# Interleaving VectorE's small dependent operations, and moving a mask sum and a residual sum to TensorE and ScalarE

## The chip, the cores and the metric

The kernel runs on one core of a Trainium2 chip. The metric is the device time of one execution in microseconds (us), lower is better. The core has TensorE (PE, with its weight loads shown as PEld), VectorE (DVE), ScalarE (ACT), GpSimd (POOL) and the DMA queue of SyncE (SP). Each engine works through its own list in order; between engines, and between dependent instructions of one engine, there are semaphores.

## The reference, cut to what matters

One adaptive-layernorm block over 16 images of 256 positions and 128 channels, all in float32:

```
h  = layernorm(x) * (1 + ca) + sa
x  = x + ga * attn(h)          # 8 heads, 33 samples around a position that the data chooses, linear interpolation
h2 = layernorm(x) * (1 + cb) + sb
logits = h2 @ router_w.T + router_b ; mask = the two largest of 8 experts
ffn = sum over chosen experts of (h2 @ expert_w[e] + expert_b[e])
x  = x + gb * ffn
```

The interpolated gather of `attn` is done as a matrix A (256 x 256 for each head and image) that VectorE builds, TensorE transposes and TensorE multiplies with h.

## The kernel before

**Units.** The 16 images are handled in nine units: one image, seven times two images, one image. `UNITS` holds them; `tiles(n)` is the number of 128-row tiles of unit n (4 for two images, 2 for one), `before(n)` the images ahead of it, `NU` = 9, `LAST` = 8, `LATE` = 7. Each engine's program is one list written out by hand: a loop over i, in which `run(i, lag, stage)` issues the stage of unit i + lag, and `second(...)` does so where the unit has two images. So in one turn of the loop three units are in work: unit i+1 is at its front (layernorm, projection, `line`, `ends_of`, `products`, `grid`), unit i in the middle (`network`, `spread_out`, `mid_A`), and units i-1 and i-2 at the back (gate and first residual, router, experts, last sum).

**VectorE in one turn.** `network` (six predicated copies that shift the rows of T by a data-dependent distance, L751) with `sum_ends` (L776) after the second copy and `masked` (hm, the expert masks times h2T, L849) and `residual` (x += gate, L805) between later ones; then for unit i+1 `line` (L694 to L702: `sums`, `f`, `lp`, `invf`, `nlf`), `ends_of` (L707 to L717: `lpe`, `fe`, `kap`) and `products` (L764, four instructions); then `spread_out(i, 0)`: two large products into AT (L788) and a small copy of the end cells (L796); `grid` (L726 to L738: `eI`, `sc`, `mask`, `sf`, `near`) of unit i+1; `route` of unit i-1 (L814 to L830: `lg`, four `max`, four `max_index`, `hit`, `mk`); `spread_out(i, 1)`; and `total(i-2)` (L854), which adds the expert result in PSUM to x.

**TensorE in one turn.** Transposes of AT (`mid_A`, L974) into four banks that ScalarE empties (L488), for image 1 of unit i-1 and then image 0 of unit i; `mid_attend` (L988); the projection rows (L946, L951); `mid_y` (L998), `mid_gate` (L1004); the experts (L1054); `back_x2T` (L1014), `back_logits` (L1025); `back_out` (L1076: transposes of the gated expert result moeT into bank pE); `back_mk` (L1031: transposes of the mask mk into pL). The end of the list, for image 0:

```python
run(i, -1, back_x2T)
run(i, -1, back_logits)
run(i, 0, mid_A, 0, 0)
run(i, -2, back_out)
run(i, 0, mid_A, 0, 1)
run(i, -1, back_mk)
run(i, 0, mid_attend, 0, 0)
run(i, 0, mid_attend, 0, 1)
```

**ScalarE in one turn.** `mid_A(i-1, 1)` (eight evictions), h^T of unit i+1 (L414), the cells c, the row activations and y between one another, then squares, sums, `front_u` (L453, waits for `nlf`), `norm2(i-1)` (L391), `back_h2T(i-1)` (L521), `back_moe(i-2)` (L537), `squares1`, `mid_A(i, 0)` (eight evictions), `back_mk(i-1)` (L530), `norm1(i+2)`.

SyncE's list has, in each turn, `masks` (the mask rows to DRAM and back, spread over 128 partitions) and `store` (a unit of x to the output), which waits for the last sum.

Of the kernel before, what the change touches and what calls it, by code (L numbers as in the profile page):

```python
# [49 lines left out]
def constants():  # L50
# [14 lines left out]
    c["erow"] = np.broadcast_to(np.arange(E, dtype=np.float32), (P, E)).copy()  # L65
# [11 lines left out]
    "late": (P, [("erow", E), ("owT", P), ("rwT", E), ("weT", E * P)]),  # L77
# [4 lines left out]
def build(nc, t):  # L82

    ctx = ExitStack()
    with ctx:
# [67 lines left out]
        hit = sb("hit", [P, BT, 2, E]); mk = sb("mk", [P, BT, NP * E])  # L153
# [29 lines left out]
        v_sum = sem("v_sum"); v_fp = sem("v_fp"); v_inv = sem("v_inv"); v_lin = sem("v_lin"); a_u = sem("a_u"); a_uR = sem("a_uR")  # L183
# [7 lines left out]
        v_top = sem("v_top"); v_topi = sem("v_topi"); v_hit = sem("v_hit"); v_mk = sem("v_mk")  # L191
        t_mk = sem("t_mk"); a_mk = sem("a_mk"); t_mb = sem("t_mb"); v_hm = sem("v_hm")
        t_moe = sem("t_moe"); a_moe = sem("a_moe"); t_out = sem("t_out"); v_out = sem("v_out")
# [65 lines left out]
        def _(sp):  # L259
# [84 lines left out]
        def _(act):  # L344
# [194 lines left out]

            for i in range(-2, LAST):  # L540
# [27 lines left out]
                run(i, -1, back_mk)  # L568
                run(i, 2, norm1)
# [21 lines left out]
        def _(dve):  # L591
# [96 lines left out]
            def line(n):  # L688
# [3 lines left out]
                if n == 0:  # L692
# [3 lines left out]
                nc.vector.tensor_scalar(f[:, 0:w], sums[:, 0:w, 0], FREQ_T / H, FREQ_MID, ALU.mult, ALU.add)  # L696
                nc.vector.scalar_tensor_tensor(lp[:, 0:w], sums[:, 0:w, 1], PHASE / H, lcol[:, 0:w], ALU.mult,
                                               ALU.add).then_inc(v_fp, 1)
                dve.wait_ge(v_fp, n + 1)
                nc.vector.reciprocal(invf[:, 0:w], f[:, 0:w]).then_inc(v_inv, 1)  # L700
# [108 lines left out]
            def route(n):  # L809
# [7 lines left out]
                for bt in range(w):  # L817
                    ins = nc.vector.max(top[:, bt, :], lg[:, bt, :])
# [368 lines left out]
```

## Time and profile before

| | |
|---|---|
| time, median of 3 runs | 310.94 us (309.18 to 311.23) |
| the profiled execution | 308.9 us, its span 307.0 us |
| busy in the span: DVE, PE, ACT, POOL | 277.2 (90%), 257.3 (84%), 229.4 (75%), 38.8 (13%) us |
| the chain that ended last, by engine | DVE 50%, PE 22%, issue 14%, ACT 11% |
| mean granted TensorE clock | 0.898 |

The profile is of one execution. The span runs from its first to its last instruction; 1.9 us of the device time lie outside it. TensorE's busy time is modelled and includes overlap of pipelined matmuls, so it isn't a measure of how full TensorE is.

### The profile page before, as it was taken

To read this page: it belongs to the slowest core of one execution; us is meant where nothing else is said; L and a number is where in the kernel's file an instruction comes from. 1 tells how busy PE (TensorE), PEld (TensorE's weight loads), DVE (VectorE), ACT (ScalarE), POOL (GpSimd) and SP (SyncE) were. 2 spreads that over 40 slices of the span, in tenths; PEclk is the share of its full clock that TensorE was granted. 3 is DMA by queue.
4 is the path that set the end of the run, shared out by engine and by line. 5 is a ranking of instruction groups with operands and counts; after the bars stand their busy time and mean duration, and the time that the engine had idled before them with its cause. 6 is when DMAs were issued, how large, how long until landed. Compare 5 with 4: busy or idle time off the path is not lost.

```text
span 307.0 us, 5136 instructions
## 1 busy us (share of the span) xinstructions
PE 257.3 (84%) x1720; PEld 189.1 (62%) x1720; DVE 277.2 (90%) x570; ACT 229.4 (75%) x636; POOL 38.8 (13%) x64
## 2 busy tenths in 40 slices
PE   6970971999489998999699989999899959888995
PEld 3530830874388477857597568747784758475664
DVE  7799988999979899999999999999999999991772
ACT  3585788799868998898869988998679656845301
POOL 6204001200410011002020011002200400001100
PEclk9596697599958999899969997999699989999999
DMA  5630000020002200140005000500003000400001
GB/s 170 206 97 0 2 0 0 0 71 1 1 2 61 96 1 0 36 138 3 0 1 174 0 0 2 168 8 1 0 37 137 2 1 20 155 0 2 26 9 53
DMA packets 12160, 12.91 MB, mean 42 GB/s; under 512 B 1171, under 2 KB 11110, under 8 KB 11366
## 3 DMA queue, kind: packets, MB, share of 16 engines
q1 hardware_dynamic: 11684, 12.18, 12.8%
q10 hardware_dynamic: 450, 0.40, 0.5%
q8 instruction: 14, 0.23, 0.3%
q14 instruction: 12, 0.10, 0.1%
HBM read 10.43 MB, written 2.15 MB: 41 GB/s over the span
## 4 chain that ended last, share of the span: by engine, by line
DVE 50%; PE 22%; issue 14%; ACT 11%; POOL 2%; DVEq 0%; ACTq 0%; POOLq 0%
DVE AT L788 18%; DVE T L751 12%; PE pT L974 4%; DVE hm L849 4%; PE pR L974 3%; PE pY L1054 3%; ACT c L471 2%; DVE x L805 2%; PE pE L1054 2%; ACT xn L391 2%; DVE endw L776 2%; PE pR L951 2%; DVE x L854 1%; ACT hT L414 1%; DVE prodF L764 1%
## 5 line engine op out<-in xcount | busy, mean ns | idle before, releaser
L751 DVE COPY_PREDICATED T<-mask,T 128x672 f32<-128x672 int16 (+11 forms) x54 | 83.3, 1543 | 0.8
L788 DVE TENSOR_TENSOR AT<-T,c 128x2064 f32<-128x2064 f32 x32 | 72.3, 2301 | 0.0
L488 ACT ACTIVATE A<-pT 128x512 f32<-128x512 f32 x64 | 36.1, 599 | 27.6 <-PE pT L974 27.1
L974 PE MATMUL pT<-first,AT 128*128 128x128 f32 x256 | 43.9, 328 | 13.1 <-DVE AT L796 13.0
L1054 PE MATMUL pE<-hm,late 128*128 128x256 f32 x224 | 52.6, 386 | 0.0
L974 PEld LDWEIGHTS pT<-first,AT 128*128 128x128 f32 x256 | 37.3, 173 | 17.2 <-DVE AT L796 15.5
L1054 PEld LDWEIGHTS pE<-hm,late 128*128 128x128 f32 x224 | 41.2, 190 | 6.6
L974 PE MATMUL pR<-first,AT 128*128 128x128 f32 x256 | 40.4, 311 | 0.0
L315 POOL TENSOR_SCALAR ve<-sq 128x4 f32<-128x4 f32 (+1 forms) x18 | 8.8, 487 | 245.8 <-ACT xn L361 202.2
L488 ACT ACTIVATE A<-pR 128x512 f32<-128x512 f32 x64 | 35.8, 611 | 3.7 <-PE pR L974 3.6
L974 PEld LDWEIGHTS pR<-first,AT 128*128 128x128 f32 x256 | 36.0, 165 | 0.0
L988 PE MATMUL pY<-A,hs 128*32 128x256 f32 x512 | 31.7, 384 | 0.2
L391 ACT ACTIVATE xn<-x,nm,rs 128x128 f32<-128x128 f32 x64 | 26.4, 480 | 5.1 <-POOL nm L319 5.1
L849 DVE TENSOR_TENSOR hm<-mkb,h2T 128x2048 f32<-128x2048 bf16 x13 | 29.7, 2284 | 0.0
L951 PE MATMUL pR<-proj,hT 128*128 128x297 f32 x64 | 25.5, 482 | 1.2 <-ACT hT L414 1.2
L471 ACT ACTIVATE c<-near,early 128x172 f32<-128x172 f32 (+1 forms) x54 | 26.0, 568 | 0.0
L988 PEld LDWEIGHTS pY<-A,hs 128*32 128x32 f32 x512 | 14.1, 109 | 13.1 <-ACT A L488 5.7
L361 ACT ACTIVATE xn<-x,mu 128x128 f32<-128x128 f32 x52 | 20.2, 390 | 0.5
L317 POOL TENSOR_TENSOR rs<-ve,mhalf 128x4 f32<-128x4 f32 (+1 forms) x18 | 19.8, 1102 | 1.5
L1014 PE MATMUL pX<-first,xn 128*128 128x128 f32 x32 | 6.1, 314 | 13.6 <-ACT xn L391 13.6
L426 ACT ACTIVATE T<-pR 128x297 f32<-128x297 f32 x32 | 13.8, 431 | 3.4 <-PE pR L951 3.4
L1025 PE MATMUL pL<-late,h2T 128*128 128x8 f32 x60 | 9.8, 289 | 7.7 <-ACT h2T L521 7.7
(139 smaller groups left out, 370.9 us busy)
## 6 DMA issues: line engine op xcount, KB each, us to landing
mkb<-mask_rows SPq DMA_DIRECT2D x6, 1024.0 KB, 5.4
x<-in_x SPq DMA_DIRECT2D x7, 256.0 KB, 5.6
out<-x SPq DMA_DIRECT2D x7, 256.0 KB, 5.7
late<-in_late SPq DMA_DIRECT2D x1, 584.0 KB, 3.9
mkb<-mask_rows SPq DMA_DIRECT2D x1, 512.0 KB, 3.8
x<-in_x SPq DMA_DIRECT2D x2, 128.0 KB, 3.5
wmod<-in_wmod ACTq DMA_DIRECT2D x1, 256.0 KB, 3.6
out<-x SPq DMA_DIRECT2D x2, 128.0 KB, 3.3
```

The costliest lines, as they stand in the source:

```text
L317: nc.gpsimd.tensor_tensor(rs[:, 0:w], ve[:, 0:w], mhalf[:, 0:w], ALU.pow).then_inc(out, 1)
L361: ins = nc.scalar.activation(junk[:, bt, :], of_x(n)[:, bt, :], ACT.Square, bias=mu[:, bt:bt + 1], accum_out=sq[:, bt:bt + 1])
L391: ins = nc.scalar.activation(xn[:, bt, :], of_x(n)[:, bt, :], ACT.Identity, bias=nm[:, bt:bt + 1], scale=rs[:, bt:bt + 1])
L471: nc.scalar.activation(cells[:, :, :, r], near[:, 0:w, :], ACT.Abs, bias=off[:, r:r + 1]).then_inc(a_abs, 1)
L488: nc.scalar.activation(A[b][:, m, 2 * j:2 * j + 2, :].rearrange("p h l -> p (h l)"), four_banks(k)[:, :], ACT.Copy).then_inc(a_A, 1)
L751: nc.vector.copy_predicated(rows[:, :, :, j0:j1], spread(mask[:, k, 0:w, j0:j1], [P, w, H, j1 - j0], 2), rows[:, :, :, j0 + (1 << bit):j1 ...
L788: nc.vector.tensor_tensor(AT[:, bt, :, :].rearrange("p h (j r) -> p h j r", r=BLK), spread(T[n % 2][:, bt, 0:H, 0:NB], [P, H, NB, BLK], 3) ...
L849: nc.vector.tensor_tensor(hm[b][:, :, :], mkb[n % 2][:, :, b * L:(b + 1) * L], spread(own, [P, E, L], 1), ALU.mult).then_inc(v_hm, 1)
L951: mm(dst, hT[:, bt * P:(bt + 1) * P], proj[:, :], start=False, stop=True).then_inc(t_row, 1)
L974: ins = nc.tensor.transpose(four_banks(k)[:, c0:c0 + P], AT[:, 2 * b + i, 2 * j + a, m * P:(m + 1) * P], ident)
L988: ins = mm(pY[32 * j:32 * j + 32, b * L:(b + 1) * L], hs[n % 2][:, 2 * b + m, hh, :], A[b][:, m, hh, :], start=(m == 0 and a == 0), stop=( ...
L1054: ins = mm(dst, weT[:, e, :], hm[b][:, e, :], start=False, stop=(e == E - 1))
```

## The change

Three things, and two series of matmuls that write nothing of use:

- **VectorE's order.** `line` takes `lpe` and `fe` in between and `invf` waits only for `f`; `grid` becomes `places`, `moves`, `stage_masks`, `offset`, `cells_from`, `route` becomes `logits`, `best`, `hits`, and the pieces of the two alternate; `spread_out` is issued tile by tile and its end copy (`set_ends`) comes one instruction later; `sum_ends` is cut in two around the second copy of `network`.
- **Hits on TensorE.** `hit` is written in three copies (24 columns in place of 8, so 128x192 elements for four tiles in place of 128x64), the addition `mk` goes, and TensorE's `back_mk` adds the two hits of a tile in the bank: two plain float32 matmuls against the identity for each tile in place of one transpose.
- **The last sum in the bank**, for units 0 to 5: `back_out` multiplies the identity with x into the bank and adds the transposed moeT there, two plain float32 matmuls for each tile in place of one transpose. ScalarE then copies the bank to x (a new `total`), and `store` and the next use of the bank wait for that copy. Units 6 to 8 keep VectorE's `total`.
- **Extra matmuls** in the loop from i = 1: four of bf16 128 x 512 between `back_x2T` and `back_logits`, two after `back_logits`, all into bank pT0, which nothing reads before `mid_A` rewrites it.

```diff
             def back_mk(n):
-                pe.wait_ge(v_mk, n + 1)
+                pe.wait_ge(v_hit, n + 1)
                 for bt in range(tiles(n)):
-                    ins = nc.tensor.transpose(pL[0:NP * E, bt * P:(bt + 1) * P], mk[:, bt, :], ident)
+                    for k in range(2):
+                        ins = mm(pL[0:NP * E, bt * P:(bt + 1) * P], hit[:, bt, k, :], ident,
+                                 start=(k == 0), stop=(k == 1))
                 ins.then_inc(t_mk, 1)
...
             def back_out(n):
                 pe.wait_ge(a_moe, before(n + 1))
                 for bt in range(tiles(n)):
-                    ins = nc.tensor.transpose(moe_bank(n)[:, bt * P:(bt + 1) * P], moeT[:, bt * P:(bt + 1) * P], ident)
+                    dst = moe_bank(n)[:, bt * P:(bt + 1) * P]
+                    if n < LATE - 1:
+                        pe.wait_ge(v_x2, n + 1)
+                        mm(dst, ident, of_x(n)[:, bt, :], start=True, stop=False)
+                        ins = mm(dst, moeT[:, bt * P:(bt + 1) * P], ident, start=False, stop=True)
+                    else:
+                        ins = nc.tensor.transpose(dst, moeT[:, bt * P:(bt + 1) * P], ident)
                 ins.then_inc(t_out, 1)
...
                 run(i, -1, back_x2T)
+                if i > 0:
+                    warm_up(4, pT[0])
                 run(i, -1, back_logits)
+                if i > 0:
+                    warm_up(2, pT[0])
                 run(i, 0, mid_A, 0, 0)
...
+            def total(n):                      # ScalarE
+                act.wait_ge(t_out, n + 1)
+                nc.scalar.activation(of_x(n), moe_bank(n)[:, 0:tiles(n) * C].rearrange("p (a c) -> p a c", c=C),
+                                     ACT.Copy).then_inc(a_out, 1)
...
                 run(i, -1, back_mk)
+                run(i, -2, total)
                 run(i, 2, norm1)
...
-                run(i, 0, network, range(0, 2))
+                run(i, 0, network, range(0, 1))
...
-                run(i, 0, sum_ends)
+                run(i, 0, sum_ends, 0)
+                run(i, 0, network, range(1, 2))
+                run(i, 0, sum_ends, 1)
                 run(i, 0, network, range(2, 4))
...
                 run(i, 1, line)
+                run(i, 1, past_ends)
                 run(i, 1, ends_of)
-                run(i, 1, products)
+                run(i, 1, product, 0, 0)
+                run(i, 1, product, 0, 1)
+                run(i, 1, product, 1, 0)
+                run(i, 1, product, 1, 1)
                 run(i, 0, spread_out, 0)
-                run(i, 1, grid)
-                run(i, -1, route)
-                second(i, 0, spread_out, 1)
-                run(i, -2, total)
+                run(i, 0, spread_out, 1)
+                run(i, 1, places)
+                run(i, 0, set_ends, 0)
+                run(i, 1, moves)
+                run(i, -1, logits)
+                run(i, 1, stage_masks)
+                run(i, -1, best)
+                run(i, 1, offset)
+                run(i, -1, hits)
+                second(i, 0, spread_out, 2)
+                second(i, 0, spread_out, 3)
+                run(i, 1, cells_from)
+                second(i, 0, set_ends, 1)
```

## Rows read from the trace of the kernel before

**Rows 1.** The page, part 1: busy us (share of the span) xinstructions.

```profile
PE 257.3 (84%) x1720; PEld 189.1 (62%) x1720; DVE 277.2 (90%) x570; ACT 229.4 (75%) x636; POOL 38.8 (13%) x64
```

**Rows 2.** Busy time by windows: stretch, length, engines, PEclk, DMA share, GB/s.

```profile
82.50:115.40 32.90, 29.50 (x198) 22.57 (x199) 29.77 (x59) 28.51 (x81) 2.87 (x6) 0.84 0.11 37
115.40:148.20 32.80, 30.88 (x217) 23.21 (x216) 32.22 (x61) 29.48 (x85) 4.13 (x6) 0.95 0.14 41
148.20:181.10 32.90, 29.46 (x205) 22.23 (x204) 32.31 (x61) 28.77 (x83) 3.17 (x6) 0.90 0.14 41
...
246.10:270.00 23.90, 19.64 (x164) 15.40 (x165) 23.45 (x38) 15.55 (x35) 0.00 (x0) 0.93 0.18 57
```

**Rows 3.** DVE's waits: us in total, times, longest us.

```profile
DVE lg L814 <- PE pL L1025: 8.1, 2, 6.4
```

**Rows 4.** DVE's timeline, one turn: start us, us, line, operation.

```profile
152.70 0.20 DVE L796 COPY AT<-endw 128x32 f32<-128x32 f32 x1
...
155.85 0.22 DVE L825 TENSOR_TENSOR hit<-late,topi 128x64 f32<-128x64 f32 x1
156.11 0.26 DVE L830 TENSOR_TENSOR mk<-hit 128x96 f32<-128x96 f32 x1
156.28 4.52 DVE L788 TENSOR_TENSOR AT<-T,c 128x2064 f32<-128x2064 f32 x2
...
160.94 0.69 DVE L854 TENSOR_TENSOR x<-pE,x 128x512 f32<-128x512 f32 x1
161.53 2.85 DVE L751 COPY_PREDICATED T<-mask,T 128x672 f32<-128x672 int16 x2
...
173.05 0.28 DVE L805 SCALAR_TENSOR_TENSOR x<-pY,x 128x128 f32<-128x128 f32 x1
...
178.00 0.18 DVE L696 TENSOR_SCALAR f<-sums 128x4 f32<-128x4 f32 x1
178.10 0.15 DVE L697 SCALAR_TENSOR_TENSOR lp<-sums,early 128x4 f32<-128x4 f32 x1
178.28 0.18 DVE L700 RECIPROCAL invf<-f 128x4 f32<-128x4 f32 x1
...
181.01 2.31 DVE L788 TENSOR_TENSOR AT<-T,c 128x2064 f32<-128x2064 f32 x1
```

**Rows 5.** PE's timeline, the same turn and the next one's start.

```profile
152.96 1.97 PE L974 MATMUL pT<-first,AT 128*128 128x128 f32 x8 [0.92 <-DVE AT L796]
...
156.43 1.06 PE L1076 MATMUL pE<-first,moeT 128*128 128x128 f32 x4
...
159.83 0.60 PE L1031 MATMUL pL<-first,mk 128*24 128x128 f32 x4
...
160.36 1.93 PE L988 MATMUL pY<-A,hs 128*32 128x256 f32 x32
...
162.22 1.09 PE L974 MATMUL pT<-first,AT 128*128 128x128 f32 x8
...
171.79 0.66 PE L1004 MATMUL pY<-first,y 128*128 128x128 f32 x4 [0.70 <-ACT y L510]
...
184.12 1.06 PE L1025 MATMUL pL<-late,h2T 128*128 128x8 f32 x8 [1.11 <-ACT h2T L521]
```

**Rows 6.** ACT's timeline, the same turn and the next one's start.

```profile
162.98 1.09 ACT L488 ACTIVATE A<-pT 128x512 f32<-128x512 f32 x2 [0.27 <-PE pT L974]
...
183.05 1.02 ACT L521 ACTIVATE h2T<-pX,modT 128x256 f32<-128x256 f32 x2 [0.75 <-PE pX L1014]
```

**Rows 7.** Busy time by windows, finer; the clock is the third number from the end.

```profile
156.40:158.04 1.64, 1.64 (x10) 1.64 (x9) 1.64 (x1) 0.61 (x2) 0.00 (x0) 0.50 0.00 0
158.04:159.68 1.64, 1.64 (x13) 1.64 (x12) 1.64 (x2) 1.12 (x3) 0.00 (x0) 0.73 0.00 0
```

**Rows 8.** PE's timeline, the end of the span.

```profile
285.13 0.61 PE L1031 MATMUL pL<-first,mk 128*24 128x128 f32 x4
```

**Rows 9.** PE's timeline, start: the nine extra matmuls that stand there.

```profile
13.12 3.31 PE L913 MATMUL pE<-warm 128*128 128x512 bf16 x9
```

More of the change, by code:

```diff
@@ new lines, in places, with moves @@
+            def places(n):
+                w = tiles(n)
+                dve.wait_ge(a_uR, n + 1)
+                nc.vector.scalar_tensor_tensor(eI[:, 0:w, :], uR[:, 0:w, :], ROUND, jcol[:, 0:w, :], ALU.subtract,
+                                               ALU.add).then_inc(v_eI, 1)
+            def moves(n):
+                nc.vector.tensor_scalar(sc[:, 0:tiles(n), :], uR[:, 0:tiles(n), 0:NB], ROUND, -float(HALF), ALU.subtract,
+                                        ALU.max).then_inc(v_sc, 1)
@@ L721, in grid, with stage_masks @@
+            def stage_masks(n):
                 w = tiles(n)
@@ L769, in sum_ends, with product @@
-            def sum_ends(n):
+            def product(n, q, far):
+                if q == 0 and not far:
+                    dve.wait_ge(v_kap, n + 1)
+                    dve.wait_ge(a_row, LT * before(n + 1))
+                own = slice(q, tiles(n), LT)
+                prod, count = ((prodN, END), (prodF, FAR))[far]
+                side = (q + far) % 2
+                c0 = SHIFT[q] + (S - count if side else 0)
+                nc.vector.tensor_tensor(
+                    prod[:, own, :, :], T[n % 2][:, own, 0:H, c0:c0 + count],
+                    spread(kap[:, own, side, 0:count], [P, UNITS[n][1], H, count], 2), ALU.mult).then_inc(v_prod, 1)
@@ L770, in sum_ends @@
+            def sum_ends(n, far):
                 w = tiles(n)
-                dve.wait_ge(v_prod, n + 1)
+                dve.wait_ge(v_prod, 4 * (n + 1))
+                if n > 0:
+                    dve.wait_ge(v_end, before(n))
                 cells = endw[:, 0:w, :, :].rearrange("p (b t) e h -> p b (t e) h", t=LT)
-                for own, prod in ((slice(0, 4, 3), prodN), (slice(1, 3), prodF)):
-                    src = prod[:, 0:w, :, :].rearrange("p (b t) h s -> p b t h s", t=LT)
-                    ins = nc.vector.tensor_reduce(cells[:, :, own, :], src, AX.X, ALU.add)
@@ L777, in sum_ends, with spread_out @@
-                ins.then_inc(v_endw, 1)
-            def spread_out(n, b):
-                img = before(n) + b
-                if b == 0:
+                own, prod = ((slice(0, 4, 3), prodN), (slice(1, 3), prodF))[far]
+                src = prod[:, 0:w, :, :].rearrange("p (b t) h s -> p b t h s", t=LT)
+                nc.vector.tensor_reduce(cells[:, :, own, :], src, AX.X, ALU.add).then_inc(v_endw, 1)
+            def spread_out(n, bt):
+                b = bt // LT
+                if bt == 0:
@@ L809, in route, with logits @@
             def route(n):
+                logits(n)
+                best(n)
+                hits(n)
+            def logits(n):
                 w = tiles(n)
```

124 lines of the change are left out of this document (59 added, 65 removed).

## The prediction

> **What bounds the kernel now.** The page's first part says VectorE: busy for 90% of the span, the others less [rows 1]. The windows of one turn of the loop say it more sharply: in the turns from 115 us on, VectorE works 32.2 of 32.8 us, so there the period is VectorE's own list [rows 2]. Not everywhere: in the turn before, it works only 29.8 of 32.9 us, and its only wait inside the loop for TensorE's logits lies there, 8.1 - 6.4 = 1.7 us [rows 2, 3]. The last turn, 246 to 270, is VectorE's again, 23.45 of 23.9 us [rows 2]. The question of this change is what comes second, and how far behind. For that I walk one turn through TensorE's and ScalarE's timelines and look where they wait for VectorE: the first transposes of a turn do (0.92 us of idle, released by the copy into AT), the gate transposes don't, they wait for ScalarE [rows 5]. So the reader should see VectorE full, and beside it a long path through two other engines that is almost as long.
>
> **What VectorE saves in a full turn.** (a) Laced dependences. `lp` starts 0.10 us behind `f`, before `f` (0.18 us) is over; `invf`, which waits for `lp`, starts 0.18 us behind it, after its end [rows 4]. So a dependence costs 0.08 to 0.1 us more than an independent follower. The new order takes the wait out of some nine places: two in `line`, the two end copies, `sf` to `near`, `lg` to `max`, `max` to `max_index`, `max_index` to `hit`, first to second copy of `network`: 9 x 0.09 = 0.8. (b) `hit` and `mk` together: from 155.85 to 156.28 is 0.43 us. The new `hit` has 192 elements; 64 take 0.22 and 96 take 0.26 us, so 1.1 ns per element gives 0.36, less 0.09 of overlap 0.27: saves 0.16 [rows 4]. (c) `total`: 160.94 to 161.53 = 0.59 us [rows 4]. Sum 1.55, and VectorE's own period falls from 32.8 to 31.25.
>
> The Trainium skill (VectorE: DVE Perf Modes, Rules for kernel authors) speaks against (a): for chained operations the drain happens regardless, so one should minimize their count and not their semaphores. The trace shows `lp` starting before `f` ends [rows 4], so I go by the row; by that rule (a) would be nothing, which is a rival below.
>
> **What TensorE gets.** Four transposes of 128x128 are half of the group at 162.22: eight in 1.09 us with the pipeline's end, 0.11 each [rows 5]. A plain float32 matmul is issued as two instructions: the four logits matmuls stand as x8, and even with eight columns each takes 1.06/8 = 0.13 [rows 5]. So one new plain matmul is two instructions of 0.11 (by the transposes' columns) to 0.13 (by the logits' weight loads), and four tiles of two matmuls are 16 instructions, 1.75 to 2.1 us, in place of four transposes at 0.11 = 0.44. I take 0.11, as the moving operand has the transposes' 128 columns. `back_mk` and `back_out` thus add 1.3 us each: +2.6 us a turn, both between the first transposes of AT and the second image's, where ScalarE waits for them. The extra matmuls: nine took 3.31 us while the clock went up, 0.35 each [rows 9]; full against half clock bounds them at some 0.21 and 0.43. The four ahead of the logits cost 0.85 to 1.7 us and lie in a gap of 1.11 us in which TensorE waits for h2T [rows 5], so hidden at full clock, +0.6 at half; the two behind add 0.4 to 0.9 ahead of the transposes of AT, where TensorE was idle 0.92 us [rows 5].
>
> **What TensorE gets back: the clock.** The transposes at 152.96 take 1.97 us for eight, those at 162.22 take 1.09 [rows 5]: the granted clock stands at 0.50 (1.2 GHz) in the windows up to 158.0 and returns at about 159 [rows 7]. Ahead of that fall TensorE had only four transposes, 1.11 us of idle, the eight-column logits and 0.92 us of idle. From 152.96 to 162.22 are 9.26 us; the same work at full clock is 32 + 4 + 4 transposes at 0.11 = 4.4 plus 1.86 of `mid_attend` = 6.2. So the half clock costs 3.0 us here, less in turns whose mean clock is 0.95 instead of 0.90 [rows 2]. The extra matmuls fill three quarters of the first gap and part of the second. I take it that this holds the clock up, as the projection and gate stretch, with one idle of 0.70 us [rows 5], never loses it; no row shows how much filling is enough, so this is the change's main risk.
>
> The Trainium skill (TensorE: Matmul & The Clock Gate, Part 4: PE-mode transpose) says that transposes don't count as busy for the clock. Here the clock comes back at 159 after six microseconds of nothing but transposes [rows 5, 7], so I don't credit the plain matmuls with holding it by their kind.
>
> **What ScalarE gets.** `total`: an eviction of 128x512, by two A evictions in 1.09 us about 0.5 us each [rows 6]. It stands ahead of `norm1`, and in TensorE's shadow: ScalarE must wait for `back_mk` and `mid_attend` anyway.
>
> **The path behind VectorE.** Let p be the start of the first transposes (152.96). With the new work at full clock, TensorE needs 32 transposes 3.5 + two stages of 1.75 + 1.86 = 8.85 us to the second image's transposes, and the first of those is ready for ScalarE 0.65 us later: p + 9.5 (before: 162.98 - 152.96 = 10.0 [rows 5, 6]). ScalarE: eight evictions, mask rows, total 0.5 and norm1 fit in that. Then
> - ScalarE's loop: from the second image's first eviction to h2T of the next turn is 183.05 - 162.98 = 20.07 us with no wait for VectorE in it; h2T to the logits' end 184.12 + 1.06 - 183.05 = 2.13; two extra matmuls 0.43; then p again. 9.5 + 20.07 + 2.56 = 32.1 [rows 5, 6].
> - The gate's loop: first eviction to gate end 172.45 - 162.98 = 9.5; then VectorE from `residual` to the next AT 181.01 - 173.05 = 7.96, less 0.24 for `line`; two tiles of AT and `eI` and the copy 4.5 + 0.3 + 0.2. 9.5 + 9.5 + 7.7 + 5.0 = 31.7 [rows 4 to 6].
> - VectorE's: 31.25.
>
> So the period is 32.1, not 31.25: of 1.55 us saved 0.7 arrive. VectorE will wait for the gate or the logits. `lg` now stands ahead of `mask`, `sf` and `near`, so those queue behind its wait for the logits; that is 1.3 us of cover gone where the logits are late.
>
> **The sum.** First two turns: no last sum in them, VectorE bound in one only, the extra matmuls at half clock: gain 0.5 (-0.5 to 2). The turn with late logits: lacing gains what the later `lg` and slow extra matmuls take, 0 (-1.5 to 1). Four full turns x 0.7 = 2.8. The last turn, where ScalarE has slack, gives VectorE's whole 1.55 and some 0.15 more from a smaller unit: 1.7. The tail is TensorE's: the mask transposes of unit 7 stand on it (285.13 [rows 8]), now +1.3 less 0.2 from `hit`, and of unit 8 with two tiles +0.6: -1.7. Total 0.5 + 0 + 2.8 + 1.7 - 1.7 = 3.3 us. The profiled execution (308.9) becomes 305.6; it lies 2.0 below the median of the timed runs, 310.94, so the forecast in their terms is 307.6. Waiting stores, one copy later, cost nothing: they land turns ahead of their next use. What moves by under 1% (3.1 us) can't be told from no change.
>
> **Rivals.**
> - *VectorE stays the bound.* If ScalarE's loop has 0.9 us more slack than my walk gives it (a stage overlaps that I laid end to end), each turn gives 1.55: five turns 7.8 + first two 1.5 + last 1.7 - tail 1.0 = 10, so 301. For: VectorE is full in every turn [rows 2]. Against: ScalarE runs 20 us with no wait for it [rows 6]. 0.24.
> - *The clock falls all the same (slower).* The new 16-instruction stages then run at half clock. With 3.4 to 6.7 us of half clock between p and the second image, the path is p + 11.2 to 12.9, ScalarE's loop 33.8 to 35.5: each of five turns 1.0 to 2.7 over the 32.8 of now, 5 to 13, tail and the first turns +1: 315 to 323. It turns against the change once more than 0.7 us are lost to the clock in a turn. For: it falls in every turn now. Against: the filled gaps. 0.22.
> - *Dear stages.* 0.13 for each instruction instead of 0.11: +0.3 for each of two stages, so the loop is 32.75 and the turns give nothing: 310.4. 0.10.
> - *No lacing.* By the page's drain rule, VectorE's own period is 32.83 - 0.75 = 32.1, the same as ScalarE's loop, and only the last and first turns lose, 1.0: 308.6. 0.04.
>
> **Chances.** Forecast 0.40 (own range 305 to 310.5, from stages at 0.11 to 0.12 and the spread of the first turns), of which 0.22 lie more than 1% below 310.94 and 0.18 within it. Faster by over 1%: 0.22 + 0.24 + 0.01 = 0.47; within 1%: 0.18 + 0.10 + 0.03 = 0.31; slower: 0.22. The range, 300.0 to 316.5, takes in the forecast, the fast rival and the near end of the slow one.
>
> **What would show it.** The granted clock between p and p + 9: near 1.00 in all turns, or the forecast is off. L1031 and L1076 with twice to four times their instructions at 0.11 each. ScalarE idle ahead of mkT by about 1 us. VectorE busy 0.8 us less than the period, its idle at `x L805` or `lg L814`. If VectorE has no idle in the turns, the fast rival holds; if eight transposes after the logits take nearly 2 us, the slow one.

## The result

| | before | after |
|---|---|---|
| time, median of 20 runs each | 309.1 us | 310.3 us |
| ratio after / before | | 1.0048 [1.0028, 1.0068] |
| the profiled execution, its span | 308.9, 307.0 us | 311.1, 309.3 us |
| mean granted TensorE clock | 0.898 | 0.928 |

The change makes the kernel 0.5% slower; the forecast was 1.1% faster. One of the 20 runs of the changed kernel took 1439.8 us and is left out of the ratio. The ratios here and below are estimates over all other runs, with 95% intervals, and not quotients of the medians. The page's first lines and its clock line (tenths of full speed in 40 slices of the span), after:

```profile
PE 273.2 (88%) x1917; PEld 199.0 (64%) x1924; DVE 267.7 (87%) x555; ACT 230.0 (74%) x642; POOL 63.5 (21%) x64
...
PEclk9576675699969999999999999999999999999999
```

Against [rows 1] VectorE lost 9.5 us of work and TensorE gained 16; they are now level. The clock stays at full speed from about 94 us on. One thing is odd: GpSimd has the same 64 instructions, and 24.7 us more of busy time.

The windows that answer to [rows 2]: the same early stretch as there (the turn with late logits now runs from 81.99 to 118.29), a full turn, and the last turn with 2.2 us of what follows it:

```profile
82.50:115.40 32.90, 28.57 (x208) 21.50 (x210) 27.88 (x44) 27.19 (x74) 8.26 (x5) 0.90 0.12 37
118.29:150.49 32.20, 31.20 (x239) 23.44 (x239) 31.03 (x59) 28.89 (x84) 7.81 (x6) 1.00 0.14 42
246.10:269.80 23.70, 21.64 (x192) 16.43 (x192) 21.57 (x36) 16.01 (x36) 0.00 (x0) 1.00 0.18 57
```

The full turn went from 32.8 to 32.2 us, and VectorE works only 31.03 of them. In the stretch of the last turn it has 2.1 us of idle time, where it had 0.45. The timeline of VectorE in a full turn, beside [rows 4]:

```profile
155.20 0.19 DVE L828 COPY AT<-endw 128x32 f32<-128x32 f32 x1
...
157.06 0.33 DVE L760 SCALAR_TENSOR_TENSOR sf<-sc,u 128x172 f32<-128x172 f32 x1
157.29 0.36 DVE L867 TENSOR_TENSOR hit<-late,topi 128x192 f32<-128x192 f32 x1
157.56 4.53 DVE L818 TENSOR_TENSOR AT<-T,c 128x2064 f32<-128x2064 f32 x2
162.00 0.34 DVE L769 TENSOR_TENSOR near<-sf,f 128x172 f32<-128x172 f32 x1
...
174.90 0.29 DVE L837 SCALAR_TENSOR_TENSOR x<-pY,x 128x128 f32<-128x128 f32 x1 [1.00 <-PE pY L1060]
...
179.88 0.17 DVE L705 TENSOR_SCALAR f<-sums 128x4 f32<-128x4 f32 x1
179.96 0.15 DVE L706 SCALAR_TENSOR_TENSOR lp<-sums,early 128x4 f32<-128x4 f32 x1
180.09 0.18 DVE L709 RECIPROCAL invf<-f 128x4 f32<-128x4 f32 x1
...
182.70 2.30 DVE L818 TENSOR_TENSOR AT<-T,c 128x2064 f32<-128x2064 f32 x1
```

The new `hit` takes the 0.36 us of the prediction, and the idle time sits where it was to sit: 1.00 us ahead of `residual`, which waits for TensorE's gate. In `line`, `invf` now starts 0.13 us behind `lp` and before its end, where it had waited for it. TensorE's timeline beside [rows 5], then its end beside [rows 8]:

```profile
155.68 1.03 PE L1030 MATMUL pT<-first,AT 128*128 128x128 f32 x8
...
157.42 0.39 PE L1139 MATMUL pE<-x,first 128*128 128x128 f32 x2
...
158.98 0.39 PE L1140 MATMUL pE<-first,moeT 128*128 128x128 f32 x2
...
161.05 1.82 PE L1089 MATMUL pL<-first,hit 128*24 128x128 f32 x15
...
164.63 1.09 PE L1030 MATMUL pT<-first,AT 128*128 128x128 f32 x8
...
285.18 1.93 PE L1089 MATMUL pL<-first,hit 128*24 128x128 f32 x16
...
296.70 1.05 PE L1089 MATMUL pL<-first,hit 128*24 128x128 f32 x8
```

With p the start of the first transposes, 155.68, the second image's start at p + 8.95 (forecast p + 8.85). From 157.42 to 159.21 stand sixteen instructions of the last sum, 1.79 us; the mask stage at 161.05 has sixteen too, of which one stands apart at 162.70. Eight transposes take 1.03 us at either place, where [rows 5] had 1.97 at half clock. ScalarE in the next turn, beside [rows 6]:

```profile
185.47 1.02 ACT L524 ACTIVATE h2T<-pX,modT 128x256 f32<-128x256 f32 x2 [0.75 <-PE pX L1070]
...
195.22 0.59 ACT L533 ACTIVATE mkT<-pL 24x512 bf16<-24x512 f32 x1 [1.10 <-PE pL L1089]
195.71 0.57 ACT L545 ACTIVATE x<-pE 128x512 f32<-128x512 f32 x1
```

And what answers to [rows 3], VectorE's waits (in total, times, longest). The wait of `hm` for the mask rows is new; that of `residual` was 1.9 us in two places before:

```profile
DVE lg L851 <- PE pL L1081: 9.3, 3, 6.4
...
DVE hm L885 <- DMA mkb<-mask_rows: 4.9, 4, 2.3
DVE x L837 <- PE pY L1060: 4.3, 5, 1.4
```

**Where the time went.** The trace is cut at the first AT product of each unit, from unit 2 on. Before: 80.00, 115.33, 148.15, 181.01, 213.83, 245.98, 267.49, end 307.0. After: 81.99, 118.29, 150.49, 182.70, 214.88, 246.01, 267.55, end 309.3. With the prediction's terms (gains positive, us):

| | forecast | measured |
|---|---|---|
| start and first two turns | +0.5 | -2.0 |
| the turn with late logits | 0 | 35.33 to 36.30: -1.0 |
| four full turns | +2.8 | 0.62 + 0.65 + 0.64 + 1.02 = +2.9 |
| the last turn | +1.7 | 21.51 to 21.54: 0.0 |
| the tail | -1.7 | 39.51 to 41.75: -2.2 |
| sum | +3.3 | -2.3 |

The first line is probably mostly chance. When the clock comes back to full speed in the first 20 us differs between executions, at 15.6 us before and 18.9 after: the nine matmuls of [rows 9] took 3.31 us before and 4.05 after. AT of unit 1 begins anywhere from 48.9 to 52.7 in the profiles of this study, whatever the edit. AT of unit 2 begins at 80.0 and 80.8 in the two profiles with the old order, and at 78.6 to 82.1, on average 80.2, in the fourteen with the new one. So the profiles show neither the forecast gain nor a loss there that is clear of chance. The timed runs of one kernel (e1 below, the mask sum back on VectorE) fall into two groups as well, two of 299.0 us at a mean clock of 0.94 and four of 301.9 to 302.6 at 0.92 to 0.93; that this is the same chance isn't shown, as only one of them was profiled. That is why full turns, most of which repeat to 0.1 us within a kernel, are compared below, and times by their intervals.

### The profile page after: what moved, and what is told of

Its sections match the earlier page's. It is cut to its first block, busy times and chain, and to the rows that moved or that the text cites. A ratio compares the mean times of both kernels' runs of the same rounds, so it can differ in the third digit from the quotient of the medians.

```text
span 309.3 us, 5550 instructions
## 1 busy us (share of the span) xinstructions
PE 273.2 (88%) x1917; PEld 199.0 (64%) x1924; DVE 267.7 (87%) x555; ACT 230.0 (74%) x642; POOL 63.5 (21%) x64
## 4 chain that ended last, share of the span: by engine, by line
PE 56%; ACT 21%; DVE 10%; issue 8%; DMA 2%; POOL 2%; ACTq 0%; DVEq 0%; POOLq 0%
PE pE L1113 11%; PE pT L1030 7%; PE pR L1030 6%; ACT A L491 5%; PE pR L1007 5%; PE pL L1089 5%; DVE AT L818 4%; ACT xn L394 3%; ACT c L474 3%; PE pL L1081 3%; PE pY L1044 3%; PE pY L1113 3%; ACT hT L417 2%; PE pT L969 2%; ACT y L513 2%
## 5 line engine op out<-in xcount | busy, mean ns | idle before, releaser
L318 POOL TENSOR_SCALAR ve<-sq 128x4 f32<-128x4 f32 (+1 forms) x18 | 7.0, 392 | 220.8 <-ACT xn L364 177.8
L491 ACT ACTIVATE A<-pT 128x512 f32<-128x512 f32 x64 | 35.0, 596 | 23.2 <-PE pT L1030 23.1
L1030 PE MATMUL pT<-first,AT 128*128 128x128 f32 x256 | 36.6, 290 | 9.3 <-DVE AT L828 9.3
L1030 PEld LDWEIGHTS pT<-first,AT 128*128 128x128 f32 x256 | 31.5, 151 | 14.9 <-DVE AT L828 10.5
L1030 PE MATMUL pR<-first,AT 128*128 128x128 f32 x256 | 34.9, 282 | 0.0
L320 POOL TENSOR_TENSOR rs<-ve,mhalf 128x4 f32<-128x4 f32 (+1 forms) x18 | 32.9, 1829 | 1.5
L1030 PEld LDWEIGHTS pR<-first,AT 128*128 128x128 f32 x256 | 30.6, 147 | 0.0
L1007 PE MATMUL pR<-proj,hT 128*128 128x297 f32 x64 | 27.5, 515 | 1.1 <-ACT hT L417 1.1
L1044 PEld LDWEIGHTS pY<-A,hs 128*32 128x32 f32 x512 | 16.1, 109 | 10.9 <-ACT A L491 4.7
L322 POOL TENSOR_TENSOR nm<-mu,rs 128x4 f32<-128x4 f32 (+1 forms) x18 | 19.4, 1076 | 1.4
L1089 PE MATMUL pL<-first,hit 128*24 128x128 f32 x128 | 15.6, 274 | 0.0
```

Source lines behind the costliest of these rows:

```text
L320: nc.gpsimd.tensor_tensor(rs[:, 0:w], ve[:, 0:w], mhalf[:, 0:w], ALU.pow).then_inc(out, 1)
L491: nc.scalar.activation(A[b][:, m, 2 * j:2 * j + 2, :].rearrange("p h l -> p (h l)"), four_banks(k)[:, :], ACT.Copy).then_inc(a_A, 1)
L1007: mm(dst, hT[:, bt * P:(bt + 1) * P], proj[:, :], start=False, stop=True).then_inc(t_row, 1)
L1030: ins = nc.tensor.transpose(four_banks(k)[:, c0:c0 + P], AT[:, 2 * b + i, 2 * j + a, m * P:(m + 1) * P], ident)
L1044: ins = mm(pY[32 * j:32 * j + 32, b * L:(b + 1) * L], hs[n % 2][:, 2 * b + m, hh, :], A[b][:, m, hh, :], start=(m == 0 and a == 0), stop=( ...
L1089: ins = mm(pL[0:NP * E, bt * P:(bt + 1) * P], hit[:, bt, k, :], ident, start=(k == 0), stop=(k == 1))
```

## The experiments

"Lacing" is VectorE's new order, the "bank" the last sum in the bank, and the "hits" the mask sum on TensorE. All against the kernel before on the same chip (its medians there: 308.7, 309.6, 309.1, 309.5 us). "Turn" is a full turn between 115 and 215 us, "last" the last turn, "tail" the time from the last unit's AT to the end, from each profile. Where two kinds of turn differ, both are given.

| kernel | time | ratio | turn | last | tail |
|---|---|---|---|---|---|
| before | 309.1 | 1 | 32.8 | 21.5 | 39.5 |
| after | 310.3 | 1.0048 | 32.2 | 21.5 | 41.8 |
| e1 mask sum on VectorE | 302.0 | 0.973 | 31.1 | 20.7 | 39.4 |
| e2 last sum on VectorE | 307.7 | 0.996 | 32.3 | 20.6 | 41.8 |
| e3 no extra matmuls | 313.3 | 1.013 | 32.05, 33.65 | 22.8 | 42.3 |
| e4 lacing alone | 303.5 | 0.981 | 31.7 | 21.7 | 39.5 |
| e5 old masks, units 7, 8 | 307.4 | 0.996 | 32.2 | 21.7 | 39.4 |
| e6 lacing, extra matmuls | 302.0 | 0.975 | 31.7 | 20.1 | 39.5 |
| e7 extra matmuls alone | 307.1 | 0.993 | 32.8 | 21.3 | 39.5 |
| e8 hits in bf16 | 303.4 | 0.980 | 31.8 | 20.7 | 39.8 |
| e9 mask stage earlier | 312.6 | 1.014 | 32.85 | 21.7 | 41.8 |
| e10 lacing, last sum in bank | 304.1 | 0.983 | 32.4, 31.1 | 23.1 | 39.4 |
| e11 e2, GpSimd's steps earlier | 306.0 | 0.990 | 31.65 | 20.9 | 41.8 |
| e12 e6, GpSimd's steps later | 304.5 | 0.986 | 32.4 | 20.1 | 39.4 |
| e13 e8, GpSimd ahead of AT | 302.5 | 0.978 | 31.15 | 21.9 | 39.9 |
| e14 e1, GpSimd ahead of AT | 300.7 | 0.972 | 31.15 | 20.5 | 39.4 |

### e1: the mask sum back on VectorE

```diff
-                nc.vector.tensor_tensor(hit[:, 0:w, :, :], ...)              # 128x192, three copies
+                nc.vector.tensor_tensor(hit[:, 0:w, :, 0:E], ...)            # 128x64
+                nc.vector.tensor_tensor(mk[:, 0:w, :], ..., ALU.add)          # first hit + second hit
...
-                    for k in range(2):
-                        ins = mm(pL[...], hit[:, bt, k, :], ident, start=(k == 0), stop=(k == 1))
+                    ins = nc.tensor.transpose(pL[...], mk[:, bt, :], ident)
```

> The changed kernel with the mask addition back on VectorE and one transpose a tile in the mask stage; all else as changed. Theory A (the longer mask stage on TensorE gives the gain back: it is 1.3 us of the path to the second image, makes the mask rows late for hm, and stands in the tail): VectorE becomes the bound of the full turns, AT to AT falls from 32.2 to 31.3 to 31.6 us, the waits of hm for mkb (4.9 us in total) vanish, the tail is 1.5 to 2 us shorter, time 301 to 304. Theory B (the early turns and the clock lose it, not the mask stage): turns stay at 32.2, time 308 to 310. Theory C (laced order saves nothing, only total was saved): turns 32.2, time 307 to 309.

Measured 302.0 us, 0.9729 [0.9671, 0.9787]. The turns are 31.1 us, VectorE's own list, and tail and last turn are shorter as well. This one part costs the changed kernel 8 us: about 1.0 in each of four turns, 1.5 in the turn with late logits, 0.8 in the last, 2.4 in the tail.

### e2: the last sum back on VectorE

```diff
-                run(i, -2, total)        # in ScalarE's list; TensorE adds x in the bank
+                run(i, -2, total)        # in VectorE's list; TensorE only transposes
```

> The changed kernel with every last sum back on VectorE and back_out as transposes; hits stay on TensorE, laced order and extra matmuls stay. Theory A (TensorE's path of two stages of 16 instructions is the bound): with one stage gone the path is 32.2 - 1.3 = 30.9 us and VectorE bounds again at 31.7 (measured for the order alone) - 0.16 = 31.5; the tail keeps its 2.3 us; time 304 to 307. If the two stages were not additive on one path, turns stay at 32.2 or rise by VectorE's 0.6 to 32.8, time 310 to 313.

Measured 307.7 us, 0.9959 [0.9929, 0.999]. Less work for TensorE, yet the turns stayed at 32.3 us. ScalarE's timeline says what it waits for, and GpSimd's why that is late:

```profile
192.91 1.65 ACT L391 ACTIVATE xn<-x,nm,rs 128x128 f32<-128x128 f32 x4 [1.84 <-POOL nm L319]
```

```profile
186.04 6.00 POOL L317 TENSOR_TENSOR rs<-ve,mhalf 128x4 f32<-128x4 f32 x1
192.12 0.68 POOL L319 TENSOR_TENSOR nm<-mu,rs 128x4 f32<-128x4 f32 x1
```

A power of 128x4 elements takes 6.00 us. In the kernel before the same instruction takes 1.01:

```profile
187.01 1.01 POOL L317 TENSOR_TENSOR rs<-ve,mhalf 128x4 f32<-128x4 f32 x1
```

There VectorE's second AT pair starts at 189.14, after GpSimd is done. Here it runs from 186.38 to 190.90, with `near` behind it until 191.15, and `rs` ends 0.9 us later. The laced order starts the second AT pair 7.1 us after the first instead of 8.1, and so on top of GpSimd's three small operations. e11 to e14 test this.

### e3: no extra matmuls

```diff
-                if i > 0:
-                    warm_up(4, pT[0])
...
-                if i > 0:
-                    warm_up(2, pT[0])
```

> The changed kernel without the six extra matmuls a turn. If these hold TensorE's clock up (my step in the prediction): the clock falls to 0.50 behind the logits in every turn, the two stages of 16 instructions run partly at half clock, AT to AT is 34 to 35.5 us, time 318 to 328. Theory B (the extra matmuls cost and the clock stays up by the plain matmuls themselves): turns 32.0 to 32.2, time 308 to 310.

Measured 313.3 us, 1.0132 [1.0069, 1.0196]: 3 us over the changed kernel, where 8 to 18 were expected. Its windows, three full turns, the granted clock third from the end:

```profile
115.99:148.04 32.05, 30.17 (x234) 22.96 (x233) 31.01 (x59) 28.91 (x84) 7.81 (x6) 1.00 0.14 42
148.04:181.68 33.64, 31.77 (x234) 24.56 (x233) 30.99 (x59) 28.96 (x84) 8.16 (x6) 0.95 0.13 40
181.68:215.34 33.66, 31.84 (x234) 24.62 (x233) 31.04 (x58) 28.90 (x82) 7.84 (x6) 0.95 0.14 41
```

The same work takes 32.05 us where the clock held by itself and 33.65 where it fell to a mean of 0.95; after had 1.00 in all of them. VectorE's work is 31.0 us in each: it is the path through TensorE that the clock stretches. Most of it arrives by way of the mask rows, for which `hm` waits 1.9 us in the two slower turns and 0.24 in the first.

### e4 and e6: lacing alone, and with the extra matmuls

e4 keeps only VectorE's new order; the three other parts are as before. e6 adds the extra matmuls.

> Only the new order of VectorE's instructions: mask addition and all last sums on VectorE, transposes in both stages, no extra matmuls. If a removed dependence is worth 0.09 us and nothing else is late: VectorE's turn is 32.8 - 0.8 = 32.0, time 303 to 305. With the path behind it still at half clock (32.3 to 32.9 in the turns with a mean clock of 0.90): 305 to 308. Theory C (laced order saves nothing): 309, no difference to before.

> The new order and the six extra matmuls, nothing of the mask and the last sum moved. If the clock stays up, the path behind VectorE is 30.5 us or less and VectorE's turn of 32.0 bounds: time 302 to 305, 0 to 3 us under the kernel with the order alone. Theory C: 308 to 310.

Measured 303.5 us, 0.9812 [0.9757, 0.9867], and 302.0 us, 0.9752 [0.9708, 0.9796]; the two intervals overlap. The turns are 31.7 us in both, against 32.8: the order alone saves 1.1 us a turn. The prediction had 0.8 from nine dependences at 0.09.

By the Trainium skill (VectorE: DVE Perf Modes, Rules for kernel authors) the drain happens for chained operations regardless, and only fewer of them help. The runs disagree with the second half: with the same 570 VectorE instructions in the trace of e4 as before, the turn fell by 1.1 us.

### e5: the old mask stage for the last two units

Units 7 and 8, whose masks lie in the tail, use VectorE's `mk` and one transpose per tile; the others keep the hits.

> The changed kernel, but the last two units (7 and 8) use the old mask: added on VectorE, one transpose a tile. It separates the tail from the turns. Theory A: turns unchanged at 32.2, the stretch from the last AT to the end 1.7 to 2.3 us shorter, time 307.5 to 309. If the tail's loss was something else: no difference.

Measured 307.4 us, 0.9963 [0.993, 0.9997]. Two of the three turns stay at 32.2 (the third, 32.5, has a wait of 1.3 us for mask rows), and the tail falls by 2.4 us to that of before: the tail's loss is the two mask stages, 1.93 and 1.05 us instead of 0.61 [rows 8] and 0.38.

### e8: hits in bf16

```diff
-        hit = sb("hit", [P, BT, 2, NP * E]);
+        hit = sb("hit", [P, BT, 2, NP * E], BF16); idb = sb("idb", [P, P], BF16)
...
-                        ins = mm(pL[...], hit[:, bt, k, :], ident,
+                        ins = mm(pL[...], hit[:, bt, k, :], idb[:, :],
```

> The changed kernel with hit and the identity of the mask stage in bf16 (0 and 1 are exact in it): a matmul is then one instruction, so the stage has 8 instead of 16, and each streams its columns once. Theory A: the stage takes 0.5 to 0.9 us instead of 1.75, the path behind VectorE falls to 31.0 to 31.3, VectorE bounds at 31.0, tail 1.5 us shorter, the DMA waits of hm mostly gone: 299.5 to 302.5. If what hurts is the hits' place on TensorE and not their length: 308 to 310.

Zeros and ones are exact in bf16. Measured 303.4 us, 0.9797 [0.9742, 0.9852]. The stage is eight instructions in place of sixteen, seven of them here and one at 191.21:

```profile
190.81 0.56 PE L1092 MATMUL pL<-idb,hit 128*24 128x128 bf16 x7
```

So most of the 8 us comes back, but the turns are 31.8 and not 31.0: GpSimd's `rs` takes 5.99 us here, and norm1 waits 0.78 us for `nm`.

### e9: the mask stage earlier in TensorE's list

Ahead of `back_out`, with mkT's copy between ScalarE's two halves of the evictions, so that the mask rows leave sooner.

> The changed kernel with the mask stage moved on TensorE from behind mid_A(i, 0, 1) to ahead of back_out, and the copy of mkT on ScalarE between the two halves of mid_A(i, 0). The path keeps its length, the mask rows leave 3 us earlier. It separates the late mask rows from the longer path. If the DMA wait of hm is what ate the gain of the last turn: that wait goes, the last turn is 1.5 to 2 us shorter, other turns 32.1 to 32.3, time 307.5 to 309. If the wait only hid something else that is late: last turn unchanged, 310.

Measured 312.6 us, 1.0137 [1.0089, 1.0185]: a miss. ScalarE's evictions and with them the gate come later, and `residual` waits 10.5 us in six places instead of 4.3 in five; the turns are 32.85. The last turn no longer waits for the mask rows, and yet it is 21.7 us, no shorter than with the wait. There the last unit's AT product waits 2.22 us instead, until ScalarE has written its c:

```profile
268.15 0.67 ACT L480 ACTIVATE c<-c 128x516 f32<-128x516 f32 x1
```

```profile
268.90 2.31 DVE L819 TENSOR_TENSOR AT<-T,c 128x2064 f32<-128x2064 f32 x1 [2.22 <-issue]
```

The trace names no releaser ("issue"), but the product waits for c in the program, and c is done at 268.82, 0.08 us ahead of it.

### e7 and e10: two more combinations

e7 is the kernel before with the six extra matmuls; e10 has lacing and the last sum in the bank, no hits and no extra matmuls.

> The kernel before with only the six extra matmuls. If VectorE's list is the bound of its turns (32.8 us), holding TensorE's clock up buys nothing there: turns 32.7 to 32.9, clock 0.95 or more in them, the time within 1% of before, at best 1 to 2 us less from the turn with the late logits and from the tail. Rival (the clock is what sets the turns in every order): turns under 32.3 us and the time 1.5% or more below.

> Interleaving and the last sum in the bank, mask sum on VectorE, no extra matmuls. With them (the run with the mask sum back) it was 302.0, turns 31.1. If the extra matmuls pay only where TensorE's list is long, this lies between: VectorE's own list is the same 31.1, TensorE's clock dips in each turn. Theory: turns 31.5 to 32.5, 303 to 308 us. Rival (the clock costs nothing while the mask sum is on VectorE): turns 31.1, 301 to 303 us.

e7: 307.1 us, 0.9931 [0.9899, 0.9963]. The turns are 32.8 us, so a faster TensorE is worth nothing where VectorE's list is the bound; the turn with late logits falls from 35.33 to 33.40. e10: 304.1 us, 0.9829 [0.9782, 0.9876], one turn of 32.4 at a clock of 0.95, then 31.1 and 31.1 at 1.00. So without the extra matmuls some turns pay and some don't, which neither theory said. Its last turn, 23.1 us at a clock of 0.85, shows in the windows (columns as in [rows 2]) beside those two:

```profile
114.52:146.89 32.37, 30.55 (x222) 23.20 (x221) 31.11 (x60) 28.96 (x84) 4.73 (x6) 0.95 0.14 42
146.89:178.00 31.11, 29.29 (x224) 21.88 (x223) 30.83 (x60) 29.10 (x85) 4.37 (x6) 1.00 0.15 44
239.38:262.48 23.10, 19.71 (x164) 15.56 (x162) 19.52 (x36) 14.80 (x33) 0.00 (x0) 0.85 0.20 59
```

In that last turn `hm` waits 3.45 us for the mask rows.

### e11 and e12: GpSimd's three operations moved

e11, on e2: ScalarE's `squares1`, for which GpSimd waits, goes ahead of `back_moe`, and VectorE's `near` ahead of the third AT product. e12, on e6: GpSimd's `rstd1` also waits for VectorE's `mk`, so that it comes up together with the AT pair.

```diff
+                run(i, 2, squares1)
                 run(i, -2, back_moe)
-                run(i, 2, squares1)
...
+                run(i, 1, cells_from)
                 second(i, 0, spread_out, 2)
```

```diff
+                if n > 2:
+                    pool.wait_ge(v_mk, n - 2)
                 rstd(n, sq1, ve1, ...)
```

> The kernel with the last sum on VectorE and the hits on TensorE (307.7 us, turns 32.2), with two steps moved so that GpSimd's three small operations end before VectorE's third AT product starts: ScalarE's squares of unit i+2 ahead of the gate of the experts, and VectorE's near ahead of the third product. Theory (GpSimd's pow is held 5 us behind VectorE's back-to-back products and norm1, then the evictions wait for it 1.8 us a turn): GpSimd's rs takes 1.0 us in the turns, norm1's wait for nm of 1.8 us goes, turns 31.3 to 31.7, 303 to 305 us. Rival (ScalarE would be waiting for TensorE's masks and second image anyway): rs takes 1.0 us, yet turns stay at 32.0 to 32.2 and the time within 0.5% of 307.7.

> The opposite edit on the fastest simple version (interleaving and extra matmuls, 302.0 us, turns 31.7): GpSimd's three operations also wait for VectorE's mask mk, so they come up just as VectorE's third AT product starts. Without any hold they would end at about 1.6 us behind mk, 1.4 us before ScalarE's norm1 wants them, and nothing changes (301 to 303 us). Theory (held until VectorE's two products end): they end some 6.2 us behind mk, norm1 starts about 3.3 us later, of which 1.1 us of ScalarE's idle time is cover, and the turns become 33.5 to 34, the time 310 to 314 us.

e11: 306.0 us, 0.9896 [0.9848, 0.9943], turns 31.65 instead of 32.3. GpSimd was still caught, one step later: `rs` is through before the pair (186.99), `nm`, 0.2 us of work, is not:

```profile
184.83 1.52 POOL L317 TENSOR_TENSOR rs<-ve,mhalf 128x4 f32<-128x4 f32 x1
186.43 5.13 POOL L319 TENSOR_TENSOR nm<-mu,rs 128x4 f32<-128x4 f32 x1
```

It began during VectorE's `sf` (186.24 to 186.55). `hit`, `near` and the AT pair (186.48, 186.74, 186.99) follow back to back, and all of them have two inputs in SBUF. norm1's wait fell from 1.84 to 0.43 us.

e12: 304.5 us, 0.9855 [0.9806, 0.9905] against 0.9752 for e6, turns 32.4 instead of 31.7. The three operations now take 6.1 us where they need 1.5, and norm1 waits 3.14 us. Counted from the start of the AT pair, norm1 comes 3.6 us later (6.51 us behind it, 2.95 in e6), and the turn paid 0.7 us of that, not the 1.8 to 2.3 expected. 1.1 us of the rest had been foreseen as ScalarE's idle time; that the other 1.8 us is slack of ScalarE's path behind VectorE's list is inferred and was not traced.

```profile
187.10 2.08 POOL L315 TENSOR_SCALAR ve<-sq 128x4 f32<-128x4 f32 x1 [8.25 <-DVE mk L868]
189.27 2.95 POOL L317 TENSOR_TENSOR rs<-ve,mhalf 128x4 f32<-128x4 f32 x1
192.30 0.93 POOL L319 TENSOR_TENSOR nm<-mu,rs 128x4 f32<-128x4 f32 x1
```

### e13 and e14: GpSimd out of the way, and its control

On e8 and on e1: `squares1` ahead of `back_moe`, and the third AT product waits for `nm`.

```diff
+                if 0 <= i <= NU - 3:
+                    dve.wait_ge(g_nm1, i + 3)
                 second(i, 0, spread_out, 2)
```

> The kernel with bf16 hits (303.4 us, turns 31.8 where 31.0 had been expected) with ScalarE's squares ahead of the gate of the experts, and VectorE's third AT product waiting for GpSimd's nm. In the bf16 run that wait would have been 1.0 us; with the squares 0.7 us earlier it is 0.1 to 0.6. Theory (in the bf16 run norm1, held with GpSimd, set the turns): rs and nm end before the product, norm1's 0.8 us wait goes, turns 31.1 to 31.5, 0.5 to 1% less than 303.4: 300.5 to 302.5 us. Rival (the 16-instruction sum stage on TensorE sets them, not GpSimd): turns 31.8 or more, since VectorE only got another wait, 303 to 305 us.

> The same two edits on the kernel with the mask sum back on VectorE (302.0 us, turns 31.1, GpSimd's nm held by 1.9 us only and norm1 not waiting for it in the turns). Theory: nothing to win there, since VectorE's own list is the bound: turns 31.1 to 31.6, 301 to 304 us. Rival (these edits shorten ScalarE's path whatever GpSimd does): turns under 31.0 and less than 300.5 us.

e13: 302.5 us, 0.9775 [0.9735, 0.9815], turns 31.15 instead of 31.8. e14: 300.7 us, 0.9724 [0.9686, 0.9761], turns 31.15, as e1's 31.1. GpSimd in e13, the AT pair beginning at 184.33:

```profile
183.01 1.01 POOL L320 TENSOR_TENSOR rs<-ve,mhalf 128x4 f32<-128x4 f32 x1
184.10 0.20 POOL L322 TENSOR_TENSOR nm<-mu,rs 128x4 f32<-128x4 f32 x1
```

Two edits, one of them an added wait on VectorE, made the turn of e8 0.65 us shorter, and the same edits did nothing for e1. So in e8 the hold on GpSimd set the turns, not the last sum's sixteen instructions on TensorE. With it gone, bf16 hits on TensorE cost nothing in the turns; they save nothing there either (31.15 both, with the hits and with `mk`).

## Why the prediction was wrong

**What held.** (1) The bound: VectorE's list, until it is shortened below 32.1 [rows 2]. (2) The path behind it: forecast 32.1 us for a full turn, measured 32.2, with the second image at p + 8.95 for p + 8.85 and VectorE's new idle time at `residual`. ScalarE's first eviction there came at p + 9.84 for 9.5, as norm1 stood in the way: mask rows, `total` and norm1 follow each other from 163.01 to 165.6, so `total` wasn't quite in TensorE's shadow. e1 shows it from the other side: with twelve of the sixteen mask instructions gone the turn is 31.1, for VectorE's forecast list of 31.25. (3) The cost of an instruction of the stages, 0.11 us: 1.79 us for sixteen. (4) The clock: held by the extra matmuls in every full turn; a turn in which it falls is 1.6 us longer (e3). The main risk did not come about. (5) `total` is worth 0.6 us of VectorE's list: 31.7 in e6, 31.1 in e1. The 1.55 us saved on that list hold in part by luck: the order gave 1.1 us for 0.8, and the hits no 0.16 that shows.

**The step that failed: "The last turn, where ScalarE has slack, gives VectorE's whole 1.55 and some 0.15 more".** It gave nothing, and ScalarE had next to no slack. Two paths beside VectorE's list ended late there. The first is the mask rows, which go to DRAM and back before `hm` can use them, and which the prediction didn't look at. VectorE and SyncE's queue in the last turn, after:

```profile
258.87 0.28 SPq L287 DMA_DIRECT2D mask_rows<-mkT  x1
260.18 0.33 SPq L291 DMA_DIRECT2D mkb<-mask_rows  x1
```

```profile
265.34 2.29 DVE L885 TENSOR_TENSOR hm<-mkb,h2T 128x2048 f32<-128x2048 bf16 x1 [2.02 <-DMA mkb<-mask_rows]
```

and before:

```profile
257.86 0.28 SPq L287 DMA_DIRECT2D mask_rows<-mkT  x1
259.16 0.33 SPq L291 DMA_DIRECT2D mkb<-mask_rows  x1
```

```profile
264.68 2.29 DVE L849 TENSOR_TENSOR hm<-mkb,h2T 128x2048 f32<-128x2048 bf16 x1
```

From the second issue to `hm` are 5.16 us after, when it waits, and 5.52 before, when it doesn't. If the transfer takes as long in both, the rows had 0.36 us to spare. VectorE now gets there 263.32 - 246.01 = 17.3 us into the turn instead of 18.7, 1.4 earlier, and the rows leave 1.0 later, behind the longer mask stage: 1.4 + 1.0 - 0.36 = 2.04, the 2.02 of the trace.

The second path is ScalarE's own. The last unit's AT product needs c, which ScalarE writes behind the second image's evictions:

```profile
266.51 0.67 ACT L480 ACTIVATE c<-c 128x516 f32<-128x516 f32 x1
```

It is done at 267.18, 21.17 us into the turn, 1.0 later than before (20.17), and the product starts at 267.55. So without the wait for the rows the turn would have been only some 0.3 us shorter, an estimate from these two times. e9 bears this out: no wait for the rows, the product waits 2.22 us for c, which its edit puts another 0.45 us later (21.62), and the turn is 21.7. With the mask sum back on VectorE both paths are shorter: in e6 nothing waits for the rows, c is done 18.8 us into the turn and the turn is 20.1; in e1 they are 1.0, 19.9 and 20.7 us. The hits aren't the only cause: e4, with neither hits nor extra matmuls and a clock of 0.84 in this turn, waits 1.41 us for the rows and stays at 21.7, while e6, at a clock of 1.00, doesn't wait. With the last sum back on VectorE (e2) the wait is 0.44.

**The turn with late logits, forecast 0, measured -1.0.** The extra wait of `lg` was foreseen, and is there: 1.76 to 2.73 us, 3.17 in e4. What was not is again the mask rows: `hm` at 106.57 waits 2.26 us for them. The six kernels with float32 hits in this turn (after, e2, e3, e5, e9, e11) take 36.1 to 36.6 us for it, with the extra matmuls or without, the laced ones without such hits 34.7 to 35.9. With the mask sum back on VectorE alone (e1) it is 34.8, a gain of 0.5 over before. I can't split the causes further.

**The tail, forecast -1.7, measured -2.2.** The mechanism was right (e5 gives it back, 2.4 us). The two stages cost 1.3 and 0.7 us, and the 0.2 that `hit` was to save there didn't come: from `lg` to the mask stage it takes 1.89 us in both kernels.

**The start, forecast +0.5, measured -2.0**: no run shows the gain of 0.5, and how much of the -2.0 is the chance named above stays open; by the timed ratio the whole change is -1.5 us, by the two profiles -2.3. So of the 5.6 us between forecast and profile, 1.7 are the last turn, 1.0 the turn with late logits, 0.5 the tail, and 2.5 lie in this open part.

**Sums of the prediction.** The base of 310.94 us was the median of three runs; twenty give 309.1, so the profiled run lay 0.2 and not 2.0 us below the typical one. The slow rival's 315 to 323 adds its 6 to 14 us to some 309, the other rivals count from 310.94. From 0.22 and 0.26 us for 64 and 96 elements follow 1.25 ns per element and 0.38 us for the new `hit`, not 1.1 and 0.36; it took 0.36.

**A rival that came half true.** *VectorE stays the bound* was to give 1.55 us a turn and 301 us. That is the kernel without the hits (e1: turns of 31.1 and 302.0 us). The prediction weighed the parts only as a bundle; taken apart, lacing is worth -1.9% (e4), the extra matmuls -0.6 to -1.0% (e4 to e6, before to e7, e10 to e1, e3 to after), the last sum in the bank 0.6 us a turn but no more than -0.2% of the time (e6 to e1), and the float32 hits +2.1% (e6 to e2) or +3.3% (e1 to after). Intervals of these ratios are about 0.5% to either side, so lacing and hits are clear of the noise, the extra matmuls hardly in one pair alone, and the last sum not. The prediction's own sum had this in it: hits save 0.16 us on VectorE and put 1.3 us on a path 0.9 us longer than VectorE's list. What the last sum costs together with the hits (e2 to after, 0.9%, at equal full turns) is seen in the trace only in part, as 0.3 us in the fourth full turn and 0.96 in the last; the rest stays open.

## What to carry to other kernels

When a list is shortened by an interleave, price each companion edit against the path behind it, alone: here the order gave 1.9%, and a mask sum moved to the second-longest path took it all back. Look for everything that had its slack measured in the cover you remove, transfers through DRAM too: one with 0.36 us to spare becomes the next wait. And when you find such a wait, look for the path that ends just behind it: e9 took the wait away and gained nothing, as the next path left only 0.3 us. And after a reorder read the durations of small operations on GpSimd: one that grows from 1.0 to 6.0 us is not slower, it is locked out by VectorE.

## What the runs showed of the hardware

**GpSimd is held by VectorE's products, through several of them.** `rs`, 128x4 elements, two inputs in SBUF, takes 1.01 us when no AT product runs and 6.00, 6.02, 5.99 us (e2, after, e8) when the pair of 128x2064 products with two SBUF inputs starts during it. After, the numbers are these:

```profile
189.43 6.02 POOL L320 TENSOR_TENSOR rs<-ve,mhalf 128x4 f32<-128x4 f32 x1
195.52 0.20 POOL L322 TENSOR_TENSOR nm<-mu,rs 128x4 f32<-128x4 f32 x1
```

```profile
189.28 0.33 DVE L760 SCALAR_TENSOR_TENSOR sf<-sc,u 128x172 f32<-128x172 f32 x1
189.51 0.36 DVE L867 TENSOR_TENSOR hit<-late,topi 128x192 f32<-128x192 f32 x1
```

Behind these two come the AT pair (189.78 to 194.31) and `near` (until 194.56), each starting before the one ahead has ended, and all with two inputs in SBUF. `rs` ends at 195.44, 0.9 us after `near`, about what it takes alone, so it looks held through the whole row of them. The handover between two products doesn't always keep GpSimd out: in e12 `ve`, which came up during the first product, ended at 189.19, 0.06 us after that product and with the second already under way. No run here shows why.

The AT products themselves take the same 2.3 us either way. `rs` is 13.1 of GpSimd's 24.7 us of new busy time, and `nm`, held in the turns before 97 us and at 221.6, is 13.4 (`ve` lost 1.7). It didn't matter in the full turns of the changed kernel, as ScalarE came to norm1 0.5 us later still (163.98, with `nm` done at 163.5). The Trainium skill (SBUF — State Buffer, Who interferes with whom) states the rule: a VectorE instruction with two SBUF inputs contends with a GpSimd instruction that reads SBUF, for a port pair that is an exclusive lock, and the order of issue decides who blocks. The trace agrees with both. `rs` began 0.35 us ahead of the products, but 0.15 behind `sf`, and in all 18 cases of about 6.0 us in these profiles `sf` was running when it began.

**A plain float32 matmul is two instructions, a bf16 one is one:** eight matmuls are sixteen instructions of 0.11 us for the float32 hits, and eight in about 0.6 us in all for the bf16 ones.
